# Reordering the opening and the last unit of a conditioning and FP8 linear kernel on one core

## Chip, cores and metric

One core of a Trainium2 chip runs the program. The metric is device microseconds of one execution; a smaller number is better. Engines are named as in the profile: PE is TensorE (PEld its weight loads), DVE is VectorE, ACT is ScalarE, POOL is GpSimd, SP is SyncE, whose queue issues the transfers.

## The reference, cut to what matters

```python
# x: 32 x 128 x 2048, fp32
W = W_sess[session_ids]; b = b_sess[session_ids]          # 8 sessions, 32 samples
xm = x * (arange(128) < channel_counts)                     # channel mask
h = gelu(einsum('bct,bch->bht', xm, W) + b)                 # 256 hidden
o = (einsum('bht,hs->bst', h, W2) + b2) * (arange(T) < seq_lens)   # 128 x 2048 per sample
w_scale = 448 / max|weight|;  w_q = fp8_e4m3(weight * w_scale)
o_scale = 57344 / max|o|;     o_q = fp8_e5m2(o * o_scale)   # maximum over all samples
out = x + (o_q @ w_q.T) / o_scale / w_scale + bias
```

Because the scale of `o` needs the maximum over all 32 samples, the second product can only begin when all of the first part is done.

## The kernel before, in words

**First stage (lines 322 to 361 of the queue, 811 to 838 of PE).** The work is cut into 64 units of 1024 time columns, two per sample. In each unit PE multiplies the session weights with the columns: `hidden(u, 0)` and `hidden(u, 1)` for the two halves of the 256 hidden rows, each as three products of split fp32 parts (`xh`, `xl` and a high and a low weight, tile `whl`) per 512 columns. ACT takes the high part of x (`split_x`, L483), POOL the rest (L441). ACT applies Gelu twice to the first half (L489, L490) and once to the second (L495), DVE forms the low part `hl` (L600). PE projects with `project0` (six products, L802) and `project1` (fp32, L807) into `ps_o`. DVE adds the bias and masks by a window of `steps` (L610) and reduces each unit to a maximum (L613, `o_max`). The result goes to DRAM (`masked_out`).

Beside it, DVE scans the weight for its maximum in pieces of 1664 columns (L632), loaded by L284 into five slots. Then the weight is scaled (ACT L506), rounded (DVE L624 and L626, POOL L448 and L450) in 43 chunks of 768 columns.

**Session weights.** For the first four samples (`DIRECT`) the raw weight of the sample's session is loaded (L275) and split on DVE (L571, L566); for sample 0 ACT makes the high part (L527). All eight sessions are also loaded once (L309, 1 MB), split by ACT (L549) and POOL (L458) and stored to `split_w` (L329); later samples load their split weight from there (L278). Each of these loads first reads the session number into a register of SP with `value_load` (L273), from the tile `sid_i`, which the first transfer of the kernel (L294) fills. The queue executes strictly in order.

**Opening.** In SP's queue stand, in order: `sid_i`, the first half of x of sample 0, `counts_i`, `ids_i`, `bs_sb`, weight 0, `b2_sb`, the second half of x, `w2_sb`, `lens_i`, weight 1, x of sample 1, weights 2 and 3, all sessions. PE runs two 512-column fp32 warming products (L750), then `hidden_bias` (L759, the biases of all samples through a one-hot), then `hidden(0, 0)`. POOL fills `steps` with two memsets (L436, L437).

**From the first stage to the second.** After the last unit DVE masks and reduces its two halves, reduces `o_max` (L679), PE spreads the maximum over the partitions (L847), DVE computes the scale (L681 to L685) and quantizes the first sample in five cuts (L692); PE turns each cut (L860) and starts the FP8 products (L866). Meanwhile POOL adds the bias to x of sample 0, loaded again (L316), in L465.

**Second stage.** 32 samples of 64 products of 512 columns on PE (L866), with quantizing, transposing transfers, evacuation (L711) and stores beside it.

## Time and profile before

| | us |
|---|---|
| median of 3 runs | 840.53 (840.3 to 843.24) |
| the profiled execution | 842.12 |
| its span in the trace | 840.30 |
| PE busy | 830.3 (99%) |
| DVE, POOL, ACT busy | 477.9, 444.1, 321.4 |
| DMA, mean over the span | 264 GB/s |

The span is what the trace shows; 1.82 us of the profiled execution's own time lie outside it. In a row of a timeline the first number is the start and the second the length in microseconds, and the bracket tells how long the engine had been idle and what released it.

### The profile page before, as it was taken

To read this page: it belongs to the slowest core of one execution; us is meant where nothing else is said; L and a number is where in the kernel's file an instruction comes from. 1 tells how busy PE (TensorE), PEld (TensorE's weight loads), DVE (VectorE), ACT (ScalarE), POOL (GpSimd) and SP (SyncE) were. 2 spreads that over 40 slices of the span, in tenths; PEclk is the share of its full clock that TensorE was granted. 3 is DMA by queue.
4 is the path that set the end of the run, shared out by engine and by line. 5 is a ranking of instruction groups with operands and counts; after the bars stand their busy time and mean duration, and the time that the engine had idled before them with its cause. 6 is when DMAs were issued, how large, how long until landed. Compare 5 with 4: busy or idle time off the path is not lost.

```text
span 840.3 us, 9984 instructions
## 1 busy us (share of the span) xinstructions
PE 830.3 (99%) x3480; PEld 472.4 (56%) x3514; DVE 477.9 (57%) x495; ACT 321.4 (38%) x337; POOL 444.1 (53%) x195
## 2 busy tenths in 40 slices
PE   8999999999999999999999999999999999999998
PEld 5766766676767767674444444444444444444444
DVE  5989998888888888888432323232323232332322
ACT  6777777889888898883000000000000000000000
POOL 3644434799999999996543232424242424242421
PEclk9999999999999999999999999999999999999999
DMA  8899997677767976656478676767777676868672
GB/s 278 325 359 421 381 342 258 235 297 279 306 253 313 351 267 250 252 207 237 153 257 279 211 276 216 270 230 257 241 246 253 234 262 224 277 212 282 214 262 101
DMA packets 73166, 222.06 MB, mean 264 GB/s; under 512 B 37418, under 2 KB 39474, under 8 KB 52786
## 3 DMA queue, kind: packets, MB, share of 16 engines
q1 hardware_dynamic: 73138, 221.71, 73.5%
q8 instruction: 15, 0.25, 0.1%
q14 instruction: 13, 0.11, 0.0%
HBM read 144.35 MB, written 69.21 MB: 254 GB/s over the span
## 4 chain that ended last, share of the span: by engine, by line
PE 98%; issue 1%; DVE 1%; DMA 0%; ACT 0%; SPq 0%; DVEq 0%
PE ps_h L866 52%; PE ps_h L787 21%; PE ps_o L807 13%; PE ps_o L802 10%; DMA counts_i<-in__lenS 0%; DVE o_sb L610 0%; PE ps_o L866 0%; PE ps_o L787 0%; PE ps_o L759 0%; PE ps_o L860 0%; PE ps_h L842 0%; DVE o_max L613 0%; ACT whl L527 0%; PE ps_h L847 0%; DVE o_sb L711 0%
## 5 line engine op out<-in xcount | busy, mean ns | idle before, releaser
L866 PE MATMUL ps_h<-wqT,x_sb 128*128 128x512 bf16 x2015 | 439.2, 378 | 1.9 <-ACT x_sb L555 0.2
L866 PEld LDWEIGHTS ps_h<-wqT,x_sb 128*128 128x128 fp8e5 x2048 | 199.7, 98 | 240.2 <-issue 0.4
L441 POOL TENSOR_TENSOR xl<-x_sb,xh 128x1024 fp32r<-128x1024 f32 x62 | 149.4, 2410 | 83.0 <-ACT xh L483 82.9
L787 PE MATMUL ps_h<-xh,whl 128*128 128x512 f32 x508 | 158.1, 433 | 0.8 <-ACT whl L527 0.7
L465 POOL TENSOR_TENSOR x_sb<-x_sb,bias_sb 128x2048 f32<-128x2048 f32 x16 | 72.3, 4516 | 146.9 <-DMA x_sb<-in_x 146.9
L465 POOL TENSOR_TENSOR h<-h,bias_sb 128x2048 f32<-128x2048 f32 x16 | 72.3, 4516 | 130.8 <-DMA h<-in_x 130.8
L711 DVE SCALAR_TENSOR_TENSOR o_sb<-ps_h,scales,h 128x512 f32<-128x512 f32 x64 | 47.8, 746 | 155.6 <-PE ps_h L866 150.7
L711 DVE SCALAR_TENSOR_TENSOR o_sb<-ps_h,scales,x_sb 128x512 f32<-128x512 f32 x64 | 47.8, 750 | 144.9 <-PE ps_h L866 140.3
L787 PEld LDWEIGHTS ps_h<-xh,whl 128*128 128x128 f32 x508 | 96.2, 190 | 48.8 <-issue 26.5
L807 PE MATMUL ps_o<-h,w_sb 128*128 128x512 f32 x256 | 120.2, 592 | 0.0
L610 DVE SCALAR_TENSOR_TENSOR o_sb<-ps_o,b_sb,steps 128x1024 f32<-128x1024 f32 (+1 forms) x65 | 82.2, 1265 | 31.4 <-PE ps_o L807 31.1
L489 ACT ACTIVATE hh<-ps_h,hbias 128x1024 fp32r<-128x1024 f32 x63 | 70.4, 1118 | 47.6 <-PE ps_h L787 47.6
L600 DVE TENSOR_TENSOR hl<-ps_h,hh 128x1024 fp32r<-128x1024 f32 x63 | 76.7, 1217 | 8.7 <-ACT ps_h L490 8.7
L787 PE MATMUL ps_h<-xl,whl 128*128 128x512 f32 x254 | 79.8, 396 | 0.0
L613 DVE TENSOR_REDUCE o_max<-o_sb 128x1 f32<-128x1024 f32 (+1 forms) x65 | 78.2, 1204 | 2.3
L448 POOL TENSOR_TENSOR ws<-ws,wc 128x768 f32<-128x768 f32 (+1 forms) x43 | 71.4, 1659 | 11.6 <-DVE wc L626 10.4
L495 ACT ACTIVATE h<-ps_h,hbias 128x1024 f32<-128x1024 f32 x64 | 71.1, 1111 | 15.8 <-PE ps_h L787 15.7
L450 POOL TENSOR_TENSOR wqT<-ws,wc 128x768 bf16<-128x768 f32 (+1 forms) x43 | 71.0, 1650 | 3.4
L807 PEld LDWEIGHTS ps_o<-h,w_sb 128*128 128x128 f32 x256 | 48.1, 188 | 36.0 <-issue 30.8
L490 ACT ACTIVATE ps_h<-ps_h,hbias 128x1024 f32<-128x1024 f32 x63 | 67.8, 1077 | 0.0
L483 ACT ACTIVATE xh<-x_sb 128x1024 fp32r<-128x1024 f32 x62 | 65.5, 1056 | 0.0
L787 PEld LDWEIGHTS ps_h<-xl,whl 128*128 128x128 f32 x254 | 48.3, 190 | 10.7
(81 smaller groups left out, 455.7 us busy)
## 6 DMA issues: line engine op xcount, KB each, us to landing
x_sb<-in_x SPq DMA_DIRECT2D x47, 1024.0 KB, 5.4
masked_out<-o_sb SPq DMA_DIRECT2D x32, 1024.0 KB, 5.3
o_in<-masked_out SPq DMA_DIRECT2D x32, 1024.0 KB, 9.0
out<-o_sb SPq DMA_DIRECT2D x31, 1024.0 KB, 5.1
h<-in_x SPq DMA_DIRECT2D x16, 1024.0 KB, 7.2
wt<-in_L_ffn_weight SPq DMA_DIRECT2D x42, 384.0 KB, 5.3
wqT<-in_L_ffn_weight SPq DMA_DIRECT2D x19, 832.0 KB, 9.0
wraw<-split_w SPq DMA_DIRECT2D x28, 256.0 KB, 4.8
```

The costliest lines, as they stand in the source:

```text
L441: pool.tensor_tensor(xl[:, u % 2, :], x_cols(u), xh[:, u % 2, :].bitcast(fp32), ALU.subtract)\
L448: pool.tensor_tensor(v, v, c, ALU.add).then_inc(w_added, 1)
L465: pool.tensor_tensor(x2[r], x2[r], bias_sb[:, :], ALU.add).then_inc(xb_ready, 1)
L495: act.activation(h1[:, u % 2, :], ps_h[:, 1, :], ACT.Gelu, bias=hbias[:, 1, b:b + 1])\
L600: dve.tensor_tensor(hl[:, u % 2, :], h0_of(u), hh[:, u % 2, :].bitcast(fp32), ALU.subtract)\
L610: dve.scalar_tensor_tensor(o_cols(u)[:, cols], ps_o[:, u % 2, cols], b2_sb[:, :], window, ALU.add, ALU.mult)\
L613: dve.tensor_reduce(o_max[:, u + k:u + k + 1], o_cols(u)[:, cols], AX.X, ALU.max, apply_absolute_value=True)\
L711: dve.scalar_tensor_tensor(y_sb[:, r, cols], bank, y_scale, x2[r][:, cols], ALU.mult, ALU.add)\
L787: mm = nc.tensor.matmul(to[:, cols], whl[:, b % DIRECT, rows], xs[:, u % 2, cols], start=(k == 0), stop=(k == 2))
L802: nc.tensor.matmul(ps_o[:, u % 2, cols], w[:, :], hs[:, u % 2, cols], start=(k == 0), stop=False)
L807: mm = nc.tensor.matmul(ps_o[:, u % 2, cols], w2_sb[:, 1, :], h1[:, u % 2, cols], start=False, stop=True)
L866: mm = nc.tensor.matmul(bank, qT[:, r, k // 2, :, k % 2], wq[:, n, k, cols], start=(k == 0), stop=(k == KT - 1))
```

## The change

- Session numbers: `value_load` reads `ids` in DRAM directly. The tile `sid_i`, its transfer and the wait for it are gone. 32 register loads are concerned.
- Five small loads leave SP's queue at the start, beside `sid_i`. `counts_i`, `ids_i` and `bs_sb` are issued by ACT before its table load, `lens_i` and `b2_sb` behind its first instruction.
- The two memsets of `steps` move from POOL to the head of DVE; the two identity tiles move ahead of the masks. `ones` gets a semaphore of its own.
- DVE makes both parts of weight 0, ahead of the low part of x; ACT's instruction L527 is gone.
- PE: two 128-column warming products more; `hidden(0, 0)` ahead of `hidden_bias`. ACT takes the high part of unit 1 before it copies the biases.
- The last unit runs by halves of 512 columns: `hidden(63, 1)` half by half, Gelu in two instructions, then `project0` and `project1` of one half and of the other.
- The maximum of all but the last half unit is reduced before the last half is masked, into one column right behind `o_sb`; the last reduction runs over the last 512 outputs and that column.
- x of sample 0 is loaded again at unit 60 instead of 62.

```diff
 def load_session_weight(b):
-    sid = sp.value_load(sid_i[0:1, b:b + 1], min_val=0, max_val=NSESS - 1)
+    sid = sp.value_load(ids.rearrange("(a b) -> a b", a=1)[:, b:b + 1], min_val=0, max_val=NSESS - 1)
...
-            sp.dma_start(sid_i[:, :], ids.rearrange("(a b) -> a b", a=1)).then_inc(sid_loaded, 16)
             load_x_part(0)
-            sp.dma_start(counts_i[:, :], counts.partition_broadcast(P)).then_inc(counts_loaded, 16)
-            sp.dma_start(ids_i[:, :], ids.partition_broadcast(NSESS)).then_inc(ids_loaded, 16)
-            sp.dma_start(bs_sb[:, :], b_sess).then_inc(bs_loaded, 16)
-            sp.wait_ge(sid_loaded, 16)
             load_session_weight(0)
-            sp.dma_start(b2_sb[:, :], b2.rearrange("(p a) -> p a", a=1)).then_inc(b2_loaded, 16)
             load_x_part(1)
             sp.dma_start(w2_sb[:, :, :], w2.rearrange("(j p) s -> p j s", p=P)).then_inc(params_loaded, 16)
-            sp.dma_start(lens_i[:, :], lens.partition_broadcast(P)).then_inc(lens_loaded, 16)
...
-                if u == UNITS - 2:
+                if u == UNITS - 4:
                     sp.wait_ge(xl_ready, UNITS - 2)
                     load_x_again(0, 0)
...
-            pool.memset(steps[:, 0:T], 1.0).then_inc(steps_ready, 1)
-            pool.memset(steps[:, T:2 * T], 0.0).then_inc(steps_ready, 1)
...
+            act.dma_start(counts_i[:, :], counts.partition_broadcast(P)).then_inc(counts_loaded, 16)
+            act.dma_start(ids_i[:, :], ids.partition_broadcast(NSESS)).then_inc(ids_loaded, 16)
+            act.dma_start(bs_sb[:, :], b_sess).then_inc(bs_loaded, 16)
             act.wait_ge(iota_ready, 1)
             act.activation(unread[:, :], time[:, 0:1], ACT.Gelu)
+            act.dma_start(lens_i[:, :], lens.partition_broadcast(P)).then_inc(lens_loaded, 16)
+            act.dma_start(b2_sb[:, :], b2.rearrange("(p a) -> p a", a=1)).then_inc(b2_loaded, 16)
             act.wait_ge(x_first[0], 16)
             act.activation(xh[:, 0, :], x_cols(0), ACT.Copy).then_inc(xh_ready, 1)
+            act.wait_ge(x_first[1], 16)
+            act.activation(xh[:, 1, :], x_cols(1), ACT.Copy).then_inc(xh_ready, 1)
             act.wait_ge(hbias_psum, 1)
...
-            act.activation(whl[:, 0, 0:HID], raw_sb[0], ACT.Copy, scale=cmask[:, 0:1]).then_inc(wh_direct, 1)
...
+            dve.memset(steps[:, 0:T], 1.0).then_inc(steps_ready, 1)
+            dve.memset(steps[:, T:2 * T], 0.0).then_inc(steps_ready, 1)
...
+            split_session_weight(0)
             dve.wait_ge(xh_ready, 1)
             dve.tensor_tensor(xl[:, 0, :], x_cols(0), xh[:, 0, :].bitcast(fp32), ALU.subtract).then_inc(xl_ready, 1)
-            low_session_weight(0)
...
-            for k, cols in enumerate(HALVES):
-                mask_o(UNITS - 1, start, k, cols)
+            mask_o(UNITS - 1, start, 0, HALVES[0])
+            scan_o(UNITS - 1, 0, HALVES[0])
+            dve.wait_ge(o_scanned, UNITS)
+            dve.wait_ge(floor_ready, 2)
+            dve.tensor_reduce(o_and_max[:, 2 * T:2 * T + 1], o_max[:, :], AX.X, ALU.max).then_inc(o_scanned, 1)
+            mask_o(UNITS - 1, start, 1, HALVES[1])
+            dve.wait_ge(o_masked, UNITS + 1)
             dve.wait_ge(o_scanned, UNITS + 1)
-            dve.wait_ge(floor_ready, 2)
-            dve.tensor_reduce(o_pmax, o_max[:, :], AX.X, ALU.max).then_inc(o_pmax_ready, 1)
+            dve.tensor_reduce(o_pmax, o_last, AX.X, ALU.max, apply_absolute_value=True).then_inc(o_pmax_ready, 1)
...
-            warm_up(WARM_START)
+            warm_up(WARM_START, BANK)
+            warm_up(WARM_START, P)
...
+            hidden(0, 0)
             hidden_bias()
-            hidden(0, 0)
             hidden(0, 1)
...
-            hidden(UNITS - 1, 1)
-            project0(UNITS - 1, HALVES)
             for cols in HALVES:
-                project1(UNITS - 1, [cols])
+                hidden(UNITS - 1, 1, [cols])
+            for k, cols in enumerate(HALVES):
+                project0(UNITS - 1, [cols])
+                project1(UNITS - 1, [cols], k)
```

## Rows read from the trace of the kernel before

**Rows 1.** The page: the chain that ended last, and PE's costliest group.

```profile
PE ps_h L866 52%; PE ps_h L787 21%; PE ps_o L807 13%; PE ps_o L802 10%; DMA counts_i<-in__lenS 0%; DVE o_sb L610 0%; PE ps_o L866 0%; PE ps_o L787 0%; PE ps_o L759 0%; PE ps_o L860 0%; PE ps_h L842 0%; DVE o_max L613 0%; ACT whl L527 0%; PE ps_h L847 0%; DVE o_sb L711 0%
...
L866 PE MATMUL ps_h<-wqT,x_sb 128*128 128x512 bf16 x2015 | 439.2, 378 | 1.9 <-ACT x_sb L555 0.2
```

**Rows 2.** The chain in order of time (start, length), first 75 us.

```profile
1.85 3.36 DMA counts_i<-in__lenS
...
7.98 5.49 PE ps_h L787 x12
...
17.83 1.72 PE ps_o L807 x4
23.71 1.72 PE ps_o L807 x4
...
53.07 1.72 PE ps_o L807 x4
...
71.38 1.72 PE ps_o L807 x4
```

**Rows 3.** The timeline of the opening, all engines.

```profile
1.41 0.38 SPq L292 DMA_DIRECT2D x_sb<-in_x  x1
...
4.07 0.38 SPq L275 DMA_DIRECT2D o_in<-in_L_cond_W_sess  x1
...
5.05 1.06 ACT L520 ACTIVATE xh<-x_sb 128x1024 fp32r<-128x1024 f32 x1 [2.81 <-DMA x_sb<-in_x]
...
6.02 0.27 DVE L583 TENSOR_SCALAR ident<-time,chan 128x128 fp8e5<-128x128 f32 x1
...
6.24 1.03 PE L759 MATMUL ps_o<-onehot,bs_sb 8*128 8x32 f32 x4 [1.00 <-DVE onehot L582]
...
7.54 0.43 SPq L270 DMA_DIRECT2D x_sb<-in_x  x1
...
9.86 1.05 PE L787 MATMUL ps_h<-xl,whl 128*128 128x512 f32 x2
...
10.66 0.53 SPq L309 DMA_DIRECT2D wqT<-in_L_cond_W_sess  x1
...
11.01 1.12 ACT L489 ACTIVATE hh<-ps_h,hbias 128x1024 fp32r<-128x1024 f32 x1 [0.76 <-PE ps_h L787]
...
14.45 0.62 PE L787 MATMUL ps_o<-xl,whl 128*128 128x512 f32 x2
...
18.88 1.91 ACT L549 ACTIVATE wqT<-wqT 128x2048 fp32r<-128x2048 f32 x1
```

**Rows 4.** Register loads by tile; the smallest DRAM load of the transfer list (KB, landing).

```profile
L273 SPq TENSOR_LOAD <-sid_i x7: 263/272/540, 3.0 to 53.1; - x7
...
b_sb<-in_L_cond_b SPq DMA_DIRECT2D x1, 0.5 KB, 2.0
```

**Rows 5.** The timeline: POOL's memset of half of `steps`.

```profile
1.64 1.80 POOL L436 MEMSET steps<- 128x2048 bf16 x1
```

**Rows 6.** SP's queue and DVE around unit 5, then the windows view there.

```profile
47.86 1.45 SPq L278 DMA_DIRECT2D wraw<-split_w  x2
...
49.36 0.44 SPq L284 DMA_DIRECT2D wqT<-in_L_ffn_weight  x1
...
55.20 1.89 DVE L632 TENSOR_REDUCE w_max<-wqT 128x1 f32<-128x1664 f32 x1 [0.69 <-DMA wqT<-in_L_ffn_weight]
...
50.00:51.00 1.00, 1.00 (x6) 0.82 (x5) 1.00 (x2) 0.66 (x1) 1.00 (x1) 1.00 0.38 100
```

**Rows 7.** The timeline from the last unit to the scale; L692's own rows (ns min/median/max).

```profile
388.09 0.75 DVE L610 SCALAR_TENSOR_TENSOR o_sb<-ps_o,b_sb,steps 128x512 f32<-128x512 f32 x1 [0.33 <-PE ps_o L807]
...
388.84 4.51 POOL L465 TENSOR_TENSOR x_sb<-x_sb,bias_sb 128x2048 f32<-128x2048 f32 x1 [1.50 <-DMA x_sb<-in_x]
...
L692 DVE TENSOR_SCALAR x_sb<-o_in,scales x5: 341/474/880, 392.6 to 394.5; 128x512 fp8e5<-128x512 f32 x3, 128x256 fp8e5<-128x256 f32 x2
```

**Rows 8.** The windows view, DMA share in the last but one column.

```profile
376.00:378.00 2.00, 2.00 (x10) 1.67 (x9) 1.97 (x4) 2.00 (x3) 1.93 (x1) 1.00 0.00 0
```

More of the change, by code:

```diff
@@ L433, in _ @@
             pool.memset(w_max[:, SCANS:SCANS + 1], EPS).then_inc(floor_ready, 1)
-            pool.memset(o_max[:, UNITS + 1:UNITS + 2], EPS).then_inc(floor_ready, 1)
-            pool.memset(ones[:, :], 1.0).then_inc(steps_ready, 1)
-            pool.memset(steps[:, 0:T], 1.0).then_inc(steps_ready, 1)
-            pool.memset(steps[:, T:2 * T], 0.0).then_inc(steps_ready, 1)
+            pool.memset(o_max[:, UNITS:UNITS + 1], EPS).then_inc(floor_ready, 1)
+            pool.memset(ones[:, :], 1.0).then_inc(ones_ready, 1)
             def split_x_rest(u):
@@ L490, in gelu0, with gelu1 @@
                 act.activation(h0_of(u), h0_of(u), ACT.Gelu, bias=hbias[:, 0, b:b + 1]).then_inc(h0_gelu, 1)
-            def gelu1(u):
+            def gelu1(u, cols=slice(0, UNIT), k=0):
                 b = u // UPB
-                act.wait_ge(h1_psum, u + 1)
-                act.activation(h1[:, u % 2, :], ps_h[:, 1, :], ACT.Gelu, bias=hbias[:, 1, b:b + 1])\
+                act.wait_ge(h1_psum, u + k + 1)
+                act.activation(h1[:, u % 2, cols], ps_h[:, 1, cols], ACT.Gelu, bias=hbias[:, 1, b:b + 1])\
                    .then_inc(h1_gelu, 1)
@@ L746, in _, with warm_up @@
             pe.sem_inc(y_psum, ONE)
-            def warm_up(count):
+            def warm_up(count, cols):
                 for k in range(count):
-                    nc.tensor.matmul(ps_o[:, 1, 0:BANK], time[:, 0:P], time[:, 0:BANK], start=True, stop=True)
+                    nc.tensor.matmul(ps_o[:, 1, 0:cols], time[:, 0:P], time[:, 0:cols], start=True, stop=True)
             pe.wait_ge(iota_ready, 1)
-            warm_up(WARM_START)
+            warm_up(WARM_START, BANK)
+            warm_up(WARM_START, P)
             def hidden_bias():
@@ L761, in hidden_bias, with hidden @@
                 last_mm.then_inc(hbias_psum, 1)
-            def hidden(u, t):
+            def hidden(u, t, halves=HALVES):
                 b = u // UPB
@@ L785, in hidden @@
                         pe.wait_ge(xl_ready, u + 1)
-                    for cols in HALVES:
+                    for cols in halves:
                         mm = nc.tensor.matmul(to[:, cols], whl[:, b % DIRECT, rows], xs[:, u % 2, cols],
@@ L834, in _ @@
             project1(UNITS - 2, HALVES)
[L835 to L836 removed]
             for cols in HALVES:
[L838 removed]
+                hidden(UNITS - 1, 1, [cols])
+            for k, cols in enumerate(HALVES):
+                project0(UNITS - 1, [cols])
+                project1(UNITS - 1, [cols], k)
             def stay_warm(count):
```

43 lines of the change are left out of this document (22 added, 21 removed).

## The prediction

> **What bounds the kernel now.** I read the chain of waits first, as shares and then in order of time, then the timeline of its three non-product stretches, then the queue's own rows. The chain is PE products: 96% of the span on four lines [rows 1]. The second stage is 439 us of products with 1.9 us of idle time [rows 1]; the change touches nothing in it, so it stays. In the first stage a unit takes 5.88 us (from 17.83 to 23.71) [rows 2], all products. The change edits these only in the last unit, and there their order, not their number. So there are three places where it can move the end: the opening, in which PE first works at 7.98 us [rows 2]; three units from 53.07 to 71.38, which take 18.31 us where three undisturbed ones take 17.64, so 0.67 of stalls [rows 2]; and the change of stages, in which PE waits for DVE's maximum and scale. Together they leave little: the opening cannot give back all of its 8 us, as the first product needs data that take 3.6 us to land after an issue (1.41 to 5.05) [rows 3].
>
> **The opening.** SP loses six small issues, of some 0.4 us each, and a wait. The first half of x, issued at 1.41, moves 0.4 earlier, so its high part begins at 4.65 instead of 5.05 and is there at 5.7 [rows 3]. The counts, on the chain from 1.85 to 5.21 [rows 2], are now issued by ACT at about 0.8, ahead of x, and land at about 4.2. That adds five issues (about 2 us) to ACT, three of them ahead of its table load; ACT is idle for 2.81 us before x lands [rows 3], so they fit, with a few tenths left; without that cover the high part begins later, and it has 0.5 to spare before the first product.
>
> The session number from DRAM is the unknown. Before, the load from SBUF took 0.27 us (0.54 the first time) [rows 4]; the smallest DRAM transfer took 2.0 us from issue to landing [rows 4]. A word read into a register has DRAM's distance in common with the second and nothing of its descriptors and completion, so I take 0.8 and keep 0.27 and 2.0 as ends. The Trainium skill (DMA: Bandwidth & Descriptors, Latency and other measured facts) gives 600 ns as the floor of such a load; by that the sum below would be 0.4 us lower, 839.5, as unit 5 holds two such loads. Runtime: NRT & Kernel Launch (The ~15µs preamble/postamble breakdown), of the Trainium skill, has register loads from HBM at 1.3 us; by that the sum would be 841.7. No row of before shows either.
>
> With 0.8, weight 0 is issued at about 3.05 instead of 4.07 [rows 3] and has landed by 5.5. DVE now begins with two memsets of `steps`. No row of before has a memset on DVE. POOL's takes 1.80 [rows 5]; a reduction on DVE takes 1.89 for 1664 columns [rows 6], 2.33 for 2048; I take POOL's, since it is the same operation, with ends of about 1 (a faster mode) and 2.33. Two from 0.75 on end at 4.35 and the two identities (0.27 each [rows 3]) at 4.9; casts, mask and one-hot took 1.0 from the landing at 5.21 to PE's 6.24 [rows 2, 3], so 5.9; the high weight is one pass over 256 columns, 0.3 at L632's rate. So PE's first product starts at about 6.2 instead of 7.98: 1.8 us. But `hidden_bias`, 1.03 us that lay in a wait until now [rows 3], stands behind `hidden(0, 0)` in a PE that works without a gap. **1.8 - 1.0 = 0.8 us** remains. Gelu of unit 0 moves from 11.01 to about 10.0 [rows 3], which agrees. What must keep up is x of sample 1 (issued at 7.54, now about 6.1) and all sessions (10.66, now about 9.8) [rows 3]: from 1.01 on there are eight issues of 0.45 and four reads, of 0.75 as at 47.86 (1.45 less two issues) [rows 6] and 0.53 more each. ACT asked for the sessions at 18.88, just when they were there, so a later landing would be late at once. The moved first instruction of POOL costs nothing either way, as POOL waits for unit 2. The 128-column warming products end near 6.1, when the data come; they cost nothing, unless data come first. Ends for the opening: 0 and 1.8.
>
> **Unit 5.** Here the same register loads stand in the way. SP waits for the store of the split weights, then reads two session numbers and issues two loads (47.86, 1.45 us for both), and only then the weight piece that DVE scans (49.36) [rows 6]. DVE stood idle 0.69 us for that piece at 55.20, and the transfer engines ran at a share of 0.38 just after it was issued [rows 6]: the queue, not bandwidth, held it. DVE has next to no slack beside the scans (busy 1.00 of 1.00 us in that window [rows 6]), and the late scan is what stalls PE by 0.67. Two loads of 0.8 instead of 0.27 delay it by **1.06 us**, and I let all of it through to PE. Ends: 0 (if the next piece, which queues for bandwidth, is no later) and 3.46 (at 2.0). The other 26 reads stand in a queue that waits longer than it works.
>
> **The change of stages.** In the new order three products and a wait for Gelu no longer stand ahead of the first half of `ps_o`, so it is ready near 387.0. DVE began it at 388.09 after 0.33 of waiting [rows 7], so it can begin at 387.76, when it is done with unit 62. After that the same five instructions follow (the small reduction only changes place, and the last covers one column more): **0.3 us**. PE's last products come without the wait for Gelu, but behind DVE that is hidden. The second term is POOL's. Its bias addition ran from 388.84 to 393.35, after 1.50 us of waiting for x, and the first 256-column cut of the quantizing took 0.88 us where the second took 0.34 [rows 7]: it ends at 393.50, right behind POOL's end. So the two exclude each other there. Issued two units earlier, into a stretch in which the transfer engines stand idle [rows 8], x is there in time; POOL begins at 387.35, when its last chunk of the loop is rounded, and ends at 391.9, before the cut at about 392.3. That gives **0.54 us**, as the turn of that cut waits for it. Ends for this place: 0.2 and 0.9. Late next are the transposed second sample and the last rounded chunk; each has over 1 us.
>
> **Sum.** -0.8 + 1.06 - 0.84 = -0.6 us, from 842.12 to 841.5 for the profiled execution (of its span of 840.30, the same amount). The median of the runs is 1.59 below the profiled execution; from it, 840.53 - 0.6 = **839.9 us**.
>
> **Rivals.** (a) *Slow register loads, slower than before.* If a DRAM read takes 1.5 us, each load costs 1.2 more. The sessions then go out at about 12.6 instead of 10.66 and ACT waits for them: the opening turns from -0.8 to about +0.6. Unit 5 costs 2.46. With -0.84: 842.7. Gains and losses balance at about 1.1 us. At 2.0 the sums are +2.5 and +3.5, so 845.7, over the bound below. For it: the loads of the sessions and of the scanned piece have no slack. Against: the same instruction takes 0.27 from SBUF. Chance 0.22, of which 0.04 for the far end.
> (b) *The piece at unit 5 does not matter, or the read is nearly as fast as from SBUF.* The loads wait for bandwidth in most of this stretch; then only the gains remain: 840.53 - 1.64 = 838.9. Chance 0.2.
> (c) *PE's clock rises earlier.* Two 512-column products took 1.05 us at 9.86 and 0.62 at 14.45 [rows 3], while the granted clock of the windows reads 1.00 throughout: the durations, not that column, show the lower of the two levels (1.2 against 2.4 GHz) until about 13. With the first data at 6.2 and warming products up to there, PE's idle stretch of 1.00 ahead of L759 and the one ahead of 7.98 go. If the clock rises several us sooner, the products and `hidden_bias` shrink by half; ACT, nearly saturated from 11 to 24 us, caps the gain of the opening at about 1.8 instead of 0.8: 838.9, and with (b) 837.9. TensorE: Matmul & The Clock Gate of the Trainium skill (The HAM clock gate) says that activity releases the throttle, which speaks for it. Chance 0.15.
> (d) *DVE's memsets are late.* At 2.33 each the masks come 1.1 later and the opening gives nothing: 840.7. VectorE: DVE Perf Modes of the Trainium skill (Zero memsets can be issued as uint32) has a memset take one cycle per element whatever the type, which speaks for this. Chance 0.13.
>
> **How the numbers follow.** Forecast 0.3, with 839.3 to 840.5 as its own range, (a) 0.22, (b) 0.2, (c) 0.15, (d) 0.13. The cases lie from 837.9 to 845.7; leaving out the far end of (a) and the joint case of (c) and (b), the range is 838.0 to 842.9. A measurement of this kernel can tell about 0.5% from no change, 4.2 us. Gains of that size would need twice the best opening; I give them 0.02. Slower by as much is the far end of (a): 0.04. The rest, 0.94, is no change that can be told.
>
> **What would show it.** Rows for `TENSOR_LOAD` on SP at 0.6 to 1.1 us; PE's first L787 near 6.2; L759 between products; first Gelu near 10; L309 issued before 10.7; an idle time of about 1.8 before the DVE scan near 55, and more than 0.67 of stalls up to there; DVE's first half of the last unit (L610) starting near 387.8; L465 ending before L692 begins, and L692's first cut at 0.34. The forecast is wrong if the register loads have rows over 1.2, if the memsets on DVE end after 5, or if PE's products at 9 us take 0.31 each.

## The result, and the profile after

The changed kernel is slower: 846.78 us (median of 10 runs, 844.37 to 849.67) against 841.38 us (median of 10 runs of the kernel before, 840.3 to 844.77, beside it). The ratio is 1.0063, 95% interval 1.0046 to 1.0081. The forecast was 839.9 us, with a range that ended at 842.9. The profiled execution took 846.25 us, with a span of 844.4 us, against 842.12 and 840.30 before. Three single executions in the sets behind this one, one of them of the kernel before, took about 1447 us at a mean granted clock of 0.557 where all others had 0.994 to 1.00; no ratio counts them, and what lowered the clock is open.

The page of the changed kernel, its chain by engine and by line, and PE's costliest group; the second line and the third answer to [rows 1]:

```profile
PE 90%; SPq 3%; DMA 3%; issue 1%; DVE 1%; ACT 1%; POOL 0%; DVEq 0%
PE ps_h L877 52%; PE ps_h L795 18%; PE ps_o L816 11%; PE ps_o L810 9%; SPq L275 2%; DMA split_w<-wqT 1%; DMA wqT<-in_L_ffn_weight 1%; DMA wqT<-in_L_cond_W_sess 1%; DVE o_and_max L609 0%; PE ps_h L853 0%; POOL xl L434 0%; DVE hl L599 0%; ACT xh L476 0%; PE ps_o L877 0%; SPq L277 0%
...
L877 PE MATMUL ps_h<-wqT,x_sb 128*128 128x512 bf16 x2015 | 439.2, 378 | 1.9 <-ACT x_sb L554 0.2
```

PE's products fell from 96% of the chain to 90%. The second stage is the same to the tenth of a microsecond: 439.2 us, 1.9 idle. A line that no row of before has holds 2% of the chain: SP's queue at L275, the read of a session number. The chain in order of time (start, length) says where; it answers to [rows 2]:

```profile
3.03 1.73 SPq L275
16.05 5.69 DMA wqT<-in_L_cond_W_sess
...
38.25 11.89 DMA split_w<-wqT
57.21 4.00 SPq L275
61.75 2.88 SPq L275
65.52 6.79 DMA wqT<-in_L_ffn_weight
```

The timeline of the opening of the changed kernel (start, length, and in the bracket the idle time before and what ended it) answers to [rows 3]:

```profile
1.34 1.76 DVE L571 MEMSET steps<- 128x2048 bf16 x1 [1.34 <-PEq L931]
...
3.27 0.91 DVE L572 MEMSET steps<- 128x1024 uint32 x1 [0.16 <-issue]
...
5.28 0.35 SPq L277 DMA_DIRECT2D o_in<-in_L_cond_W_sess  x1
...
5.70 1.06 ACT L519 ACTIVATE xh<-x_sb 128x1024 fp32r<-128x1024 f32 x1 [2.13 <-DMA x_sb<-in_x]
...
7.40 0.35 DVE L566 TENSOR_SCALAR whl<-o_in,cmask 128x256 fp32r<-128x256 f32 x1 [2.11 <-DMA o_in<-in_L_cond_W_sess]
...
7.81 2.08 PE L795 MATMUL ps_h<-xh,whl 128*128 128x512 f32 x4 [1.71 <-DVE whl L566]
...
16.05 0.44 SPq L304 DMA_DIRECT2D wqT<-in_L_cond_W_sess  x1
16.09 1.05 PE L795 MATMUL ps_o<-xl,whl 128*128 128x512 f32 x2
...
17.61 0.63 PE L810 MATMUL ps_o<-hh,w2h 128*128 128x512 f32 x2
...
21.76 1.92 ACT L548 ACTIVATE wqT<-wqT 128x2048 fp32r<-128x2048 f32 x1 [0.52 <-DMA wqT<-in_L_cond_W_sess]
```

Weight 0 is issued at 5.28, later than the 4.07 of before, and DVE waits for it until 7.40. The first product starts 0.17 us earlier than before (7.81), after 1.71 us in which PE is idle; before, `hidden_bias` lay there. Pairs of 512-column products take 1.05 us until 16.09, the lower of the clock's two levels, and 0.63 only from 17.61; before, 0.62 at 14.45. All sessions go out at 16.05 instead of 10.66.

The rows of the register loads (ns min/median/max, first and last start) answer to [rows 4]:

```profile
L275 SPq TENSOR_LOAD <-in_itok_B_ptr x32: 822/1132/4003, 1.5 to 351.6; - x32
L275 SPq TENSOR_LOAD <-in_itok_B x32: 452/462/2876, 3.0 to 352.8; - x32
```

This is the row that the forecast didn't have. A number read from the kernel's input in DRAM is not one load but two, one behind the other: by the names in the rows first the address of the tensor (`_ptr`), then the value. The pair takes 1.6 us by the medians, 3.3 us for the first, and 6.9 us for the one at 57.21, in a queue in which the old load took 0.27. The long ones stand together: the address took 4.00, 3.38, 2.33 and 2.22 us at 57.2, 68.9, 81.2 and 92.3, and never over 1.6 from 95 us on. In the timeline around units 5 to 7 SP issues nothing at all from 57.2 to 65.11, and DVE's scans run late:

```profile
52.05 2.95 SPq L280 DMA_DIRECT2D wraw<-split_w  x2
...
59.72 1.89 DVE L633 TENSOR_REDUCE w_max<-wqT 128x1 f32<-128x1664 f32 x1 [1.70 <-DMA wqT<-in_L_ffn_weight]
...
65.11 0.36 SPq L280 DMA_DIRECT2D wraw<-split_w  x1
...
72.33 1.89 DVE L633 TENSOR_REDUCE w_max<-wqT 128x1 f32<-128x1664 f32 x1 [1.46 <-DMA wqT<-in_L_ffn_weight]
...
77.94 1.17 PE L795 MATMUL ps_h<-xh,whl 128*128 128x512 f32 x4 [0.63 <-DVE hl L599]
```

The pair of issues at 52.05 took 2.95 us where it took 1.45 [rows 6], and DVE waited 1.70 for its piece instead of 0.69. The piece behind the long read was issued at 65.52 and scanned from 72.33, after 1.46 us of waiting; the mask and the low part `hl` stand behind the scan on DVE, and PE waits for them at 77.94. The chain above runs the same way, from the two reads to the piece. At the change of stages, on the timeline:

```profile
392.58 4.53 POOL L458 TENSOR_TENSOR x_sb<-x_sb,bias_sb 128x2048 f32<-128x2048 f32 x1
...
392.65 0.74 DVE L609 SCALAR_TENSOR_TENSOR o_and_max<-ps_o,b_sb,steps 128x512 f32<-128x512 f32 x1
...
398.38 1.47 PE L877 MATMUL ps_h<-wqT,x_sb 128*128 128x512 bf16 x6 [0.17 <-ACT x_sb L554]
```

and L699's own row, the quantizing, whose first cuts are the shortest (ns min/median/max):

```profile
L699 DVE TENSOR_SCALAR x_sb<-o_in,scales x36: 346/1278/1279, 397.2 to 814.4; 128x2048 fp8e5<-128x2048 f32 x31, 128x512 fp8e5<-128x512 f32 x3, 128x256 fp8e5<-128x256 f32 x2
```

From the mask of the last unit's first half (388.09 [rows 7]; now 392.65) to the first FP8 product, 6.26 us before (to 394.35), it now takes 5.73. POOL's addition has no wait for x in front of it, and the shortest row is 0.35: the first cut of 256 columns, which had taken 0.88.

Where the time stands can be read from one kind of row, the start of each unit's projection on PE's timeline. The table gives it minus the same unit of the profiled execution of before, in us; positive is later. The last columns are the first FP8 product and the span. Each line is one execution, so it places the loss; the sizes are taken from the ratios.

| kernel | unit 0 | 2 | 6 | 7 | 10 | 20 | FP8 | span |
|---|---|---|---|---|---|---|---|---|
| changed | +2.26 | +2.83 | +2.82 | +3.51 | +5.10 | +5.29 | +4.03 | +4.1 |
| e1_after_sbuf | +2.22 | +2.24 | +2.23 | +3.20 | +2.65 | +2.64 | +1.37 | +1.4 |
| e2_before_dram | +0.26 | +6.10 | +6.09 | +5.99 | +7.16 | +7.15 | +6.94 | +7.3 |
| e3_before_stage | -1.21 | -0.86 | -0.87 | -0.31 | +0.10 | +0.09 | -1.15 | -1.2 |
| e4_open_dram | +1.76 | +2.99 | +3.07 | +2.98 | +3.45 | +3.44 | +2.20 | +3.7 |
| e5_bias_first | -1.51 | -1.14 | -1.14 | -1.25 | -1.80 | -1.81 | -2.97 | -2.7 |
| e6_before_reload | +0.05 | +0.07 | +0.06 | +0.99 | +1.98 | +2.17 | +1.67 | +1.7 |
| e7_warm_fill | -1.28 | -0.90 | -0.83 | -0.92 | -1.43 | -1.24 | -2.52 | -1.1 |
| e8_scan_first | +2.10 | +3.00 | +3.07 | +5.12 | +4.60 | +4.79 | +3.52 | +3.8 |
| e9_stage_scan | -1.22 | -1.16 | -1.16 | -0.37 | -0.89 | -0.69 | -1.97 | -2.0 |
| e10_bias_warm | -2.09 | -1.57 | -1.49 | +0.00 | -0.05 | +0.14 | -1.12 | -0.6 |
| e11_bias_warm_scan | -2.28 | -1.75 | -1.68 | -1.22 | -1.80 | -1.80 | -3.07 | -2.7 |
| e12_after_warm | -1.28 | +2.94 | +2.94 | +3.81 | +5.24 | +5.24 | +3.97 | +4.9 |
| e13_small_in_sp | -2.03 | -0.93 | -0.94 | -1.05 | -1.63 | -1.64 | -2.91 | -1.2 |
| e14_small_late | -1.56 | -1.16 | -1.09 | +0.03 | -0.48 | -0.29 | -1.56 | -0.2 |
| e15_best_again | -1.11 | -1.10 | -1.11 | -0.12 | -0.70 | -0.71 | -1.99 | -0.7 |
| e16_sbuf_small_late | -2.74 | -0.36 | -0.37 | -0.10 | +0.47 | +0.46 | -0.80 | -0.5 |
| e17_small_sp_scan | -2.26 | -1.70 | -1.63 | +1.88 | +1.32 | +1.31 | +0.03 | +0.3 |
| e18_best_again | -2.17 | -1.27 | -1.20 | -1.28 | -1.80 | -1.61 | -2.88 | -2.9 |

For the changed kernel: +2.83 by unit 2, another 2.3 between units 6 and 10, and -1.3 from unit 20 to the first FP8 product. All kernels with the new change of stages show -1.2 to -1.3 in that last step.

### The profile page after: what moved, and what is told of

Read it like the earlier page. It is cut to its first block, busy times and chain, and to the rows that moved or that the text cites. A ratio compares the mean times of both kernels' runs of the same rounds, so it can differ in the third digit from the quotient of the medians.

```text
span 844.4 us, 10056 instructions
## 1 busy us (share of the span) xinstructions
PE 833.0 (99%) x3484; PEld 474.2 (56%) x3518; DVE 479.6 (57%) x498; ACT 321.3 (38%) x337; POOL 441.3 (52%) x193
## 4 chain that ended last, share of the span: by engine, by line
PE 90%; SPq 3%; DMA 3%; issue 1%; DVE 1%; ACT 1%; POOL 0%; DVEq 0%
PE ps_h L877 52%; PE ps_h L795 18%; PE ps_o L816 11%; PE ps_o L810 9%; SPq L275 2%; DMA split_w<-wqT 1%; DMA wqT<-in_L_ffn_weight 1%; DMA wqT<-in_L_cond_W_sess 1%; DVE o_and_max L609 0%; PE ps_h L853 0%; POOL xl L434 0%; DVE hl L599 0%; ACT xh L476 0%; PE ps_o L877 0%; SPq L277 0%
## 5 line engine op out<-in xcount | busy, mean ns | idle before, releaser
L877 PE MATMUL ps_h<-wqT,x_sb 128*128 128x512 bf16 x2015 | 439.2, 378 | 1.9 <-ACT x_sb L554 0.2
L458 POOL TENSOR_TENSOR x_sb<-x_sb,bias_sb 128x2048 f32<-128x2048 f32 x16 | 73.2, 4572 | 144.2 <-DMA x_sb<-in_x 144.2
L458 POOL TENSOR_TENSOR h<-h,bias_sb 128x2048 f32<-128x2048 f32 x16 | 72.2, 4513 | 131.4 <-DMA h<-in_x 131.4
L718 DVE SCALAR_TENSOR_TENSOR o_and_max<-ps_h,scales,h 128x512 f32<-128x512 f32 x64 | 47.8, 747 | 155.5 <-PE ps_h L877 150.6
L718 DVE SCALAR_TENSOR_TENSOR o_and_max<-ps_h,scales,x_sb 128x512 f32<-128x512 f32 x64 | 47.9, 751 | 144.8 <-PE ps_h L877 140.3
L609 DVE SCALAR_TENSOR_TENSOR o_and_max<-ps_o,b_sb,steps 128x1024 f32<-128x1024 f32 (+1 forms) x65 | 82.2, 1264 | 31.4 <-PE ps_o L816 31.3
L614 DVE TENSOR_REDUCE o_max<-o_and_max 128x1 f32<-128x1024 f32 x64 | 77.5, 1212 | 2.2
L489 ACT ACTIVATE h<-ps_h,hbias 128x1024 f32<-128x1024 f32 (+1 forms) x65 | 71.3, 1098 | 16.1 <-PE ps_h L795 16.1
```

The source lines that it names most:

```text
L458: pool.tensor_tensor(x2[r], x2[r], bias_sb[:, :], ALU.add).then_inc(xb_ready, 1)
L489: act.activation(h1[:, u % 2, cols], ps_h[:, 1, cols], ACT.Gelu, bias=hbias[:, 1, b:b + 1])\
L609: dve.scalar_tensor_tensor(o_cols(u)[:, cols], ps_o[:, u % 2, cols], b2_sb[:, :], window, ALU.add, ALU.mult)\
L614: dve.tensor_reduce(o_max[:, u + k:u + k + 1], o_cols(u)[:, cols], AX.X, ALU.max, apply_absolute_value=True)\
L718: dve.scalar_tensor_tensor(y_sb[:, r, cols], bank, y_scale, x2[r][:, cols], ALU.mult, ALU.add)\
L877: mm = nc.tensor.matmul(bank, qT[:, r, k // 2, :, k % 2], wq[:, n, k, cols], start=(k == 0), stop=(k == KT - 1))
```

## The experiments

All ratios are to the kernel before, run in the same set; sets differ by up to 1.3 us in the median of before (841.4 to 842.7). The time in front of a ratio is the median of that kernel's runs, and the ratio can differ by up to 0.001 from the quotient of the two medians. "The change" is the whole diff.

### The DRAM reads alone, and the change without them

e1_after_sbuf, the change with the session numbers read from the SBUF tile again (with its transfer and its wait):

```diff
-    sid = sp.value_load(ids.rearrange("(a b) -> a b", a=1)[:, b:b + 1], ...)
+    sid = sp.value_load(sid_i[0:1, b:b + 1], ...)
```

> The changed kernel with one thing undone: the session numbers come from the SBUF tile again, whose transfer stands first in SP's queue, with the wait before weight 0. Theory A (the two dependent DRAM reads per session number, 1.27 to 6.9 us together instead of 0.27, are the whole loss): 4.0 us of span come back and the gain of the stage change (1.28) shows, so a ratio to the kernel before of about 0.997 (839 us), the first projection of unit 0 at or before 17.7, no stall over 0.4 in units 7 to 10. Theory B (the loss lies in the order of the opening: memsets at DVE's head, biases behind the first products, small loads in ACT's queue): the first projection stays near 19.9 and the time near 843. Theory C (the clock rises late because PE's early work lies elsewhere): products still at 0.5 us apart at 15 us of the span.

e2_before_dram, the reverse edit in the kernel before:

> The kernel before with DRAM reads of the session numbers alone (no tile, no transfer, no wait). Theory A: the loss alone, some 4 to 6 us: ratio 1.005 to 1.007, unit 0's projection 2 us or more later than 17.67 and 2 us more of stalls in units 7 to 10. Theory B: under 2 us in all, as weight 0 and x are issued at about the same time as before.

e4_open_dram, the change with DRAM reads for the first four samples only, SBUF for the 28 later ones:

> The changed kernel with DRAM reads for the first four samples alone; the later ones come from the SBUF tile, loaded behind the sessions. Splits the loss of theory A by place: units 7 to 10 give back their 2.3 us, the opening keeps its 2.8 late: about 844 us, ratio 1.003. If instead the stalls of units 7 to 10 stay, they come from the late opening (transfers pushed together) and not from the reads there.

Measured: e1 843.63 us, 1.0015 (1.0002 to 1.0029); e2 849.32, 1.0086 (1.0066 to 1.0106); e4 844.50, 1.0022 (1.0011 to 1.0033). So by the ratios the reads are worth 4.0 us in the changed kernel (1.0063 - 1.0015 of 842), most of it in the 28 later ones (1.0063 against 1.0022; 0.6 us for the first four), and alone they cost 7.2 us. These sizes are uncertain by some 2 us, as the intervals and the two sets allow; up to the first FP8 product the profiled executions show 2.7 us between the changed kernel and e1 and 1.8 between it and e4. Rows of e2's timeline show the path in the opening: the sessions go out 6.9 us later than before, and ACT waits 3.65 us for them:

```profile
17.52 0.44 SPq L305 DMA_DIRECT2D wqT<-in_L_cond_W_sess  x1
...
23.46 1.92 ACT L545 ACTIVATE wqT<-wqT 128x2048 fp32r<-128x2048 f32 x1 [3.65 <-DMA wqT<-in_L_cond_W_sess]
```

ACT's split of the sessions then stands in front of its own Gelu, and PE is 6.10 us late at unit 2. But e1, with no DRAM read in it, is still slower than before, and loses 2.2 us by unit 0. Its opening on the timeline:

```profile
3.76 0.36 SPq L279 DMA_DIRECT2D o_in<-in_L_cond_W_sess  x1
...
7.39 0.35 DVE L570 TENSOR_SCALAR whl<-o_in,cmask 128x256 fp32r<-128x256 f32 x1 [2.24 <-DMA o_in<-in_L_cond_W_sess]
...
7.80 2.08 PE L799 MATMUL ps_h<-xh,whl 128*128 128x512 f32 x4 [1.70 <-DVE whl L570]
...
16.08 1.05 PE L799 MATMUL ps_o<-xl,whl 128*128 128x512 f32 x2
```

Weight 0 is issued 1.5 us earlier than in the changed kernel and arrives at the same time, 3.6 us after its issue instead of 2.1. Two questions follow: does the idle time of 1.70 us with its low clock cost the 2.2 us, and what holds weight 0?

### The idle stretch ahead of the first product

e7_warm_fill is e1 with six 128-column warming products instead of two, which fill the stretch; e5_bias_first is e1 with `hidden_bias` back in it:

```diff
-            warm_up(WARM_START, P)
+            warm_up(WARM_START + 4, P)          # e7
...
-            hidden(0, 0)
             hidden_bias()
+            hidden(0, 0)                        # e5
```

> The changed kernel with the session numbers from SBUF and six 128-column warming products instead of two, which fill PE's gap from 6.1 to 7.8 us. Theory C (the lower clock lasts to 17 us because of that gap): products at 0.23 us apart from 8 to 13 us on, first projection of unit 0 two us sooner than 19.9, ratio about 0.999. Rival: the clock rises by chance of the execution whatever the gap: median unchanged at 1.0015.

> The changed kernel with the session numbers from SBUF, and the biases' products ahead of hidden(0, 0) again, as in the kernel before. The version without this last edit ran at 1.0015 of the kernel before although it has the faster stage change (0.9988 alone), so its opening costs about 2.3 us. Theory B1 (the four bias products, 1.06 us, stand in the way of PE where they lay in a gap before, and the gap they leave lets the clock rise late): most of that comes back, ratio about 0.999 or less, first projection of unit 0 at 17.7 or before. Rival B2 (DVE's memsets or ACT's queue are the reason): it stays at 1.0015.

Measured: e7 841.24, 0.9992 (0.9976 to 1.0008); e5 841.22, 0.9990 (0.9977 to 1.0003). Either takes back the loss of e1, 2.0 us, without weight 0 being a tenth earlier. The intervals just touch that of e1, which is of another set, but two different edits give the same and the table shows it in place, at unit 0. In e7 the first four products run at the higher level:

```profile
7.79 1.26 PE L799 MATMUL ps_h<-xh,whl 128*128 128x512 f32 x4
```

So the moved `hidden_bias` did not only cost its own 1.03 us: without it PE stood idle, and the products behind it ran at the lower level for some 4 us longer than before.

e10_bias_warm puts both together, e5 with two 128-column products between `hidden_bias` and `hidden(0, 0)`. e12_after_warm is the changed kernel, DRAM reads kept, with e7's six warming products:

> The changed kernel with session numbers from SBUF, the biases ahead of hidden(0, 0), and two more 128-column warming products between the two, so that PE has no gap from 1.46 us to its first data. If theory C holds (gaps before 8 us decide when the clock rises) products run at 0.23 us from about 8 us on and the opening gains up to 1.5 us more than with the biases first alone (ratio 0.999): 0.9975. If ACT, nearly saturated up to 24 us, caps the gain, the ratio stays at 0.999.

> The changed kernel as it is, DRAM reads kept, with six 128-column warming products instead of two. If the loss is two independent parts (reads 4.0 us, late clock 2.0 us), filling the gap alone takes 2 us off: ratio 1.0040. If the late transfers of the opening hide it (x of sample 1 and all sessions are issued late by the reads), under 1 us comes back: 1.0055 or more.

Measured: e10 841.55, 0.9990 (0.9981 to 1.0000), no better than e5: it leads by 1.49 us at unit 6 and has given it all back at unit 7, in this execution behind a scanned piece for which DVE waited 2.77 us. e12 847.65, 1.0068 (1.0053 to 1.0084), no better than the change itself, though its clock is up at once:

```profile
7.79 1.25 PE L795 MATMUL ps_h<-xh,whl 128*128 128x512 f32 x4 [0.80 <-DVE whl L566]
...
16.25 0.44 SPq L304 DMA_DIRECT2D wqT<-in_L_cond_W_sess  x1
...
21.89 1.92 ACT L548 ACTIVATE wqT<-wqT 128x2048 fp32r<-128x2048 f32 x1 [3.31 <-DMA wqT<-in_L_cond_W_sess]
```

Unit 0 is 3.5 us earlier than in the changed kernel and unit 2 is not: ACT waits 3.31 us for the sessions instead of 0.52. The two losses of the opening do not add; the later of the two counts, and in the changed kernel the late sessions stand right behind the slow products.

### What holds weight 0

In e13_small_in_sp (e1) all five small loads are back at their places in SP's queue. In e14_small_late (on e11, below) and e16_sbuf_small_late (on e1) only the lengths and the last bias move, behind ACT's second high part:

```diff
-            act.dma_start(lens_i[:, :], lens.partition_broadcast(P)).then_inc(lens_loaded, 16)
-            act.dma_start(b2_sb[:, :], b2.rearrange("(p a) -> p a", a=1)).then_inc(b2_loaded, 16)
             ...
             act.activation(xh[:, 1, :], x_cols(1), ACT.Copy).then_inc(xh_ready, 1)
+            act.dma_start(lens_i[:, :], lens.partition_broadcast(P)).then_inc(lens_loaded, 16)
+            act.dma_start(b2_sb[:, :], b2.rearrange("(p a) -> p a", a=1)).then_inc(b2_loaded, 16)
```

> The changed kernel with the session numbers from SBUF, and the five small loads back at their old places in SP's queue, so that ScalarE issues none. Against the version with SBUF numbers alone (first product 7.80, weight 0 issued 3.76, landed 7.39; ratio to before 1.0015). Theory A (small loads beside x slow the landing): weight 0, issued near 4.1, lands by 6.7, and the first product starts near 6.9 or as soon as the masks are there. Theory B (the halves of x set it): landing at 7.3 to 7.6 again, first product near 7.8, ratio 1.000 to 1.003.

> The fastest version so far (biases first, two more warming products between, scanned piece ahead of the session weights, SBUF numbers), with the lengths and the last bias issued by ScalarE behind its second high part of x (near 9 us) instead of near 2.1. Theory A: x lands before 4.9 instead of 5.20 and weight 0 before 6.9 instead of 7.14. Theory B: both within 0.1 of the earlier version. The lengths are needed only near 17 us, so nothing is late. Time as the version without the move, ratio to before 0.997 to 0.999.

> The changed kernel with the session numbers from SBUF, and the lengths and the last bias issued by ScalarE behind its second high part of x. If those two loads alone held weight 0, it lands at 5.8 as in e14_small_late, the first product starts at 6.1 to 6.2 (the 6.2 of the prediction), right behind the warming products, and the products run at the higher level of the clock from there or shortly after; projection of unit 0 1.5 to 2.5 us earlier than before, part of it given back where ScalarE or the session weights bind; ratio to before 0.998 to 1.000. If the clock stays low until 17 us as in the version with SBUF numbers alone, unit 0 is less than 0.5 earlier and the ratio is 1.000 to 1.002.

e13's first product on its timeline:

```profile
6.63 1.25 PE L799 MATMUL ps_h<-xh,whl 128*128 128x512 f32 x4 [0.53 <-DVE whl L570]
```

e14's weight 0, asked for at the same time as in e1:

```profile
3.76 0.36 SPq L279 DMA_DIRECT2D o_in<-in_L_cond_W_sess  x1
...
5.76 0.35 DVE L570 TENSOR_SCALAR whl<-o_in,cmask 128x256 fp32r<-128x256 f32 x1 [0.61 <-DMA o_in<-in_L_cond_W_sess]
```

and e16's first product:

```profile
6.38 1.18 PE L799 MATMUL ps_h<-xh,whl 128*128 128x512 f32 x4 [0.55 <-DVE whl L570]
```

Theory A held for the weight once those two loads are not in ScalarE's queue ahead of it: DVE begins with it 2.0 us after its issue in e14 (5.76, where e11 has 7.14) and 2.1 in e16 (5.90, where e1 has 7.39). For x it fell: ACT begins the high part at 5.08 in e14 (5.20 in e11) and at 5.18 in e16 (5.00 in e1). Measured: e13 840.42, 0.9993 (0.9980 to 1.0006); e14 841.66, 1.0000 (0.9989 to 1.0011); e16 841.69, 0.9987 (0.9972 to 1.0002). e16 is e1 with two lines moved and takes 2.4 us off it (1.0015 to 0.9987). e14 misses its forecast of 0.997 to 0.999: in its order the warming products, `hidden_bias` and two more warming products stand ahead of the first product, which starts at 7.89 with the weight long there, at the lower level; and between units 6 and 7, where it loses another 1.1 us, ACT waited 2.52 us for a split weight. e16 leads by 2.74 us at unit 0 and by 0.36 at unit 2: ACT waits 1.68 us for the sessions there. Which of the two loads does it, and where in the transfers, was not separated.

### The scanned piece at unit 5 and after

Four kernels load the piece that DVE scans ahead of the session weights in SP's queue:

```diff
             for u in range(...):
+                if u < SCANS:
+                    if u >= SLOTS:
+                        sp.wait_ge(w_scanned, u - SLOTS + 1)
+                    load_scan(u)
                 for n in range(DIRECT, B):
                 ...
-                if u < SCANS:
-                    ...
```

e8_scan_first on the change, e9_stage_scan on e3, e11_bias_warm_scan on e10, e15_best_again e11 once more:

> The changed kernel, DRAM reads kept, with the load of each scanned weight piece ahead of the session weights in SP's queue. Theory A says that the reads of units 5 and 7 (1.3 to 6.9 us each) act through what stands behind them in the queue, first the scanned piece, then x: the stalls of units 7 to 10 (2.3 us over those of before) fall to under 1 us, ratio 1.003 to 1.004. Rival (bandwidth decides when pieces land): no change, 1.006.

> The kernel before with the change of stages and the scanned piece ahead of the session weights. The stage change alone gave 0.9988. If the late piece is what stalls units 7 to 10 of the kernel before (0.67 us), the ratio comes to about 0.998; if bandwidth decides, it stays at 0.9988.

> The same with the scanned piece ahead of the session weights. It gave 0.0005 on the kernel before with SBUF numbers and moved the wait from the piece to weight 4 with DRAM numbers. Expected 0.9970, the version to beat both; if the store of the split weights is delayed as with DRAM numbers, no better than without it.

> The same program as e11_bias_warm_scan (0.9981, 0.9971 to 0.9992), measured again. If its gain is real, the ratio lies between 0.997 and 0.999 with an interval under 1; if it was chance of one set, the interval holds 1.

Measured: e8 845.70, 1.0043 (1.0030 to 1.0056); e9 840.88, 0.9983 (0.9969 to 0.9996); e11 840.62, 0.9981 (0.9971 to 0.9992); e15 841.34, 0.9993 (0.9984 to 1.0002). In e8's profiled execution the piece no longer waits on PE's path, but something else takes its place, the first split weights out of `split_w`:

```profile
58.95 0.72 ACT L507 ACTIVATE whl<-wraw,cmask 128x512 fp32r<-128x512 f32 x1 [3.47 <-DMA wraw<-split_w]
...
59.72 1.20 PE L795 MATMUL ps_h<-xh,whl 128*128 128x512 f32 x4 [1.86 <-ACT whl L507]
```

e9's 0.9983 is 0.0005 under e3's 0.9988, in another set and with overlapping intervals: the forecast 0.998, but not told apart from no gain. e11 and e15 are one program and differ by 0.0012, and their profiled executions differ in the opening, by rows of the same instruction:

```profile
7.55 1.24 PE L799 MATMUL ps_h<-xh,whl 128*128 128x512 f32 x4 [0.61 <-DVE whl L570]
```

in e11, and in e15:

```profile
7.86 1.85 PE L799 MATMUL ps_h<-xh,whl 128*128 128x512 f32 x4 [1.16 <-DVE whl L570]
```

so the interval of e11 lies under 1 and that of e15, which overlaps it, does not: a gain of 0.1 to 0.2% found in one set needs a second one.

### The change of stages

e3_before_stage is the kernel before with the last unit by halves, the early maximum and the reload at unit 60; e6_before_reload has the reload alone:

```diff
-                if u == UNITS - 2:
+                if u == UNITS - 4:
                     sp.wait_ge(xl_ready, UNITS - 2)
```

> The kernel before with the change of stages alone: last unit by halves, maximum beside the last outputs, x of sample 0 loaded again at unit 60. Theory A: the first turn of a cut comes 1.2 to 1.3 us sooner after unit 62, ratio 0.9985. Rival: the gain seen in the changed kernel comes only from its later arrival at this place (transfers and POOL had more time), then 0 to 0.5 us here.

> The kernel before with x of sample 0 loaded again at unit 60 alone. Theory: POOL's bias addition ends before the first cut of the quantizing, whose instruction falls from 0.88 to 0.34 us: 0.54 us from this edit, and DVE's first mask of the last unit still waits for PE. Rival: the cut is long for another reason (its first use of the scale), then it stays at 0.88.

Measured: e3 841.01, 0.9988 (0.9974 to 1.0001), 1.0 us; e6 842.41, 0.9996 (0.9985 to 1.0007). Their timelines show POOL's addition, in e3 and then in e6. Neither row has a wait for x in front of it, where POOL had waited 1.50 us before, and in both the addition ends before DVE's first cut begins:

```profile
387.40 4.53 POOL L467 TENSOR_TENSOR x_sb<-x_sb,bias_sb 128x2048 f32<-128x2048 f32 x1
```

```profile
389.46 4.54 POOL L465 TENSOR_TENSOR x_sb<-x_sb,bias_sb 128x2048 f32<-128x2048 f32 x1
...
394.81 1.41 DVE L692 TENSOR_SCALAR x_sb<-o_in,scales 128x256 fp8e5<-128x256 f32 x4 [0.17 <-DVE scales L685]
```

From unit 20 to the first FP8 product e3 gains 1.24 us and e6 0.50: the reload is worth the 0.54 predicted, the halves and the early maximum 0.7. e2, which has no edit here, gains 0.21, and shows why: its addition ran until 400.29, 0.51 us into the first cut, which took 0.66; before it was 0.73 into a cut of 0.88. In both the cut ends 0.15 behind the addition. e6 shows a warning too: same code as before up to unit 60, and yet 1.9 us more in units 6 to 10 of its profiled execution.

### A version that beats both

e17_small_sp_scan is e13 with the scanned piece first, that is: the change, with session numbers from SBUF, the small loads in SP's queue where they were, and the load of the piece ahead of the session weights. e18_best_again is the same program in another set:

> e13_small_in_sp (all five small loads back in SP's queue, first product 6.63, units from the second on 1.1 to 1.6 us ahead of before) with the load of the scanned piece ahead of the session weights in the queue. If the piece's lateness costs what is left in units 5 to 8, the ratio falls to 0.997 to 0.9985 with an interval under 1; if it was already hidden there (its own trace shows no stall from unit 2 to 20), it stays at 0.999.

> The same program as e17_small_sp_scan, measured again. If its 0.9975 holds apart from what differs between two sets (0.0012 between e11 and e15), the ratio is between 0.9965 and 0.9987 and its interval lies under 1; if it was chance, the ratio is 0.9990 or more, as in e13_small_in_sp.

Measured: e17 840.11 us against 842.09, 0.9975 (0.9965 to 0.9986); e18 839.82 against 842.14, 0.9979 (0.9968 to 0.9990). Both intervals lie under 1: 1.9 us less than before and 7 us less than the changed kernel. e18's first product:

```profile
6.57 1.25 PE L799 MATMUL ps_h<-xh,whl 128*128 128x512 f32 x4 [0.54 <-DVE whl L570]
```

e17's forecast had asked whether the piece still costs anything; its profiled execution loses 3.5 us between units 6 and 7 and e18's none, while the ratios agree. In e17 ACT waited 3.37 us there for the split weights, as in e8, and in e18 0.38. Units 6 to 10 vary too much from execution to execution for one trace to price them, and what loading the piece first is worth by itself is not shown: against e13 (0.9993, 0.9980 to 1.0006) the intervals still overlap.

## Why the prediction was wrong

Term by term, from the two profiled executions: the opening came to +2.8 us by unit 2 where -0.8 was predicted, the stretch of unit 5 and the units behind it to +2.5 (unit 6 to 20) where +1.06 was, and the change of stages to -1.26 where -0.84 was. That adds up to +4.0; the ratio, of ten runs each, gives +5.3. Another 0.85 us of the distance from 839.9 to 846.78 is the base: 840.53 was the median of three runs, 841.38 that of ten.

**The session number from DRAM.** This is the step that failed: "A word read into a register has DRAM's distance in common with the second and nothing of its descriptors and completion, so I take 0.8 and keep 0.27 and 2.0 as ends." The rows show two loads, and the second starts only when the first is over: 1.13 and 0.46 us by the medians, up to 4.0 and 2.9. The median pair, 1.6, lies within the ends; the first (3.3) and the one at unit 7 (6.9) do not, and these stood on the chain. Both figures of the Trainium skill that the prediction cites, 600 ns (DMA: Bandwidth & Descriptors, Latency and other measured facts) and 1.3 us (Runtime: NRT & Kernel Launch, The ~15µs preamble/postamble breakdown), are below the measured pair of 1.6; the larger is the nearer. Rival (a) had the mechanism, with its two places (late sessions, late piece) and its point of balance at 1.1 us, but its far end of 2.0 gave 845.7 and the kernel takes 846.8: one price for every read could not hold the 6.9 us of the one that mattered most. What made that one long is not shown. The transfer engines were busy at a share of 1.00 during its address, but at 1.06 and 1.04 during addresses of 0.88 (at 50.2) and 0.82 us (at 104.0). e1 and e2 show that the reads cost several us on either side.

**"The other 26 reads stand in a queue that waits longer than it works."** It failed for sample 6, whose read comes next behind those of unit 5: SP was held by one number from 57.21 until the issue at 65.11, while the piece and the x of the next units stood behind it. Where a queue has slack on average, one long read can still use it all. Between e4 and the changed kernel, which differ in the 28 later reads, two of them unit 5's, lie 0.4%.

**"The opening, -0.8."** The sign was wrong: +2.2 by unit 0 even without DRAM reads (e1). The term has three parts. Weight 0 was to be issued at about 3.05 (by the prediction's own price of a read, behind x's issue at 1.01, it is about 2.7; nothing hung on it, as the masks were to be ready at 5.9) and to have landed by 5.5. The first pair of reads held it until 5.28. And the landing came near only with the lengths and the last bias out of its way (issued at 3.76, begun with at 5.76 in e14); with them in ScalarE's queue at 2.14 and 2.53 DVE had it at 7.4 whether it was issued at 3.76 (e1) or at 5.28. The five issues had been costed as ACT's time, which did fit, and not as transfers beside weight 0. The first product "at about 6.2" is what e16 shows, 6.38. And the clock was treated as rival (c), as a gain that might come; that the same edit could lose it was not there. With the weight late, the reordered products left PE idle where `hidden_bias` had been, and the lower level lasted to about 17 us instead of 13. e7 and e5 fill the stretch and get 2 us back. One smaller part failed too: x was to be there at 4.65 and was at 5.70. In e2, which issues it at the same time but keeps the small loads in SP's queue, it is there at 4.66.

**Unit 5, +1.06.** Where it was placed it came out well: the two issues took 2.95 instead of 1.45, and DVE's wait 1.70 instead of 0.69, 1.0 us more. By unit 7 PE had lost 0.69 us more than before; of the other 1.8 up to unit 20 PE lost 1.6 in units 7 to 10, where the chain runs through the reads at 57.21 and 61.75. And the stall of PE was put down to this piece alone; with it loaded first (e8) the split weights were late instead; the ratio went from 1.0063 to 1.0043, with intervals that overlap.

**The change of stages, -0.84.** Right in kind and a little small: -1.24 in e3, -1.26 in the changed kernel. POOL's term (0.54) was right, 0.50 in e6, and so was what it rested on: the cut of DVE and the addition of POOL exclude each other there, and without the overlap the first cut fell from 0.88 to 0.35. DVE's start was predicted at 0.3 earlier, limited by unit 62's own work; that work itself moved, as before DVE had waited 0.24 us in unit 62 behind its register load of `start_i` (1.41 us from 383.3, and what follows it in the queue until 385.0), which the profile calls "issue".

**Rivals (b) and (c).** (b) fell with the same rows: the piece mattered, and no read was near 0.27. (c) went the other way in this kernel, as told above; that the clock can rise sooner is shown by e12, whose first products take 1.25 us for four, and there the late sessions took the gain.

**Rival (d)** fell: the two memsets took 1.76 and 0.91, and DVE was done with masks and one-hot at 5.3, two microseconds before it had a weight. The prediction cites a rule of the Trainium skill, VectorE: DVE Perf Modes (Zero memsets can be issued as uint32), for this rival. The trace agrees with it, but that speaks against the rival for the half of zeros: it went out as 1024 elements of uint32 instead of 2048 of bf16, at the same 0.9 ns per element (0.86 and 0.89), so in half the time.

**The signs of the prediction's own list.** Register loads over 1.2 us were named as what would make it wrong, and the pairs take 1.6 by the medians. The other two such signs did not come: DVE's memsets ended at 4.18, and PE's products at 9.7 us took 0.52 each. First product near 6.2: 7.81. First Gelu near 10: 12.02. Sessions before 10.7: 16.05. L458 done before the quantizing: it was done at 397.11, the quantizing began at 397.17, and its first cut took 0.35 where 0.34 was predicted.

## What to carry to other kernels

A register load from a kernel's input in DRAM showed as two reads, one behind the other, of 1.6 us together by the medians and 6.9 at worst; in a queue that executes in order everything behind it pays, so a small index table was better loaded into SBUF first. A small load moved to another engine's queue costs that engine's time, and it can also delay transfers beside it: follow the landing of the first critical one, not only the issues. In an opening, work that fills PE's wait is not free to move: here it left an idle engine with the lower clock behind it, and filler products in its place took the loss back.

## What the hardware showed that was not expected

- The pair of loads, and its spread: 0.82 to 4.00 us for the address and 0.45 to 2.88 for the value in one execution. In the other three kernels with 32 such pairs the longest address took 5.91 (e2), 4.61 (e8) and 5.62 us (e12). The same numbers from SBUF in the kernel before: 0.27 by the median, and 1.08 at most over all 32.
- Two small loads in ScalarE's queue, of 128 partitions each, lengthened the landing of a 128 KB load, issued in SP's queue at 3.76, from 2.0 to 3.6 us, and left that of the 512 KB load beside it alone; issued at 5.28, in the changed kernel, the 128 KB took 2.1. In the changed kernel itself x, issued at 1.00 instead of 1.41, was there 0.65 us later (5.70); with the numbers from SBUF it was there at 5.00. What delays it there was not separated.
- The clock's rise is not fixed by the program: e3 has the opening of the kernel before and was 1.21 us ahead at unit 0; e11 and e15 are one program and 1.2 us apart there. In seven traces with an idle stretch of 0.5 to 0.9 ahead of the first product (e10, e11, e12, e13, e16, e17, e18) it ran at the higher level at once, in the four with 1.6 to 1.7 (changed, e1, e4, e8) the first unit's products ran at the lower level until 16 us or later, in e4 after some at the higher. But e5, with 0.70, and e14, with none, began at the lower level too, and in e3, which differs from the kernel before only in its last units, `hidden_bias` already took 0.60 instead of 1.03; so idle time alone doesn't settle it.
